# Entropy-model transfers with 16 rows outermost, and a result step moved behind the attention maxima

## What is computed

```python
# layer 0: attention over positions; c = 192, q and k have 24 channels
q, k, v = prelu(conv1x1(gn(x), w))            # three weights
score = softmax(einsum('bnc,bcm->bnm', q, k), axis=2)
x = x + einsum('bnm,bmc->bnc', score, v)      # "x2" below
# layer 1: an entropy model, per channel, on lower = gn(x) - 0.5 and upper = gn(x) + 0.5
for i in range(4):                             # 1 -> 3 -> 3 -> 3 -> 1 hidden values per channel
    logits = softplus(m[i]) @ logits + b[i]
    if i < 3: logits = logits + tanh(f[i]) * tanh(logits)
sign = -sign(lower + upper)
x = x + max(abs(sigmoid(sign * upper) - sigmoid(sign * lower)), 1e-6)
```

## Time and profile before

| | before |
|---|---|
| median of 3 runs | 5420.98 us |
| the profiled execution | 5410.94 us |
| its span on the core | 5409.1 us |
| PE busy | 84% |
| DVE busy | 80% |
| ACT busy | 67% |
| POOL busy | 18% |
| mean DMA rate | 56 GB/s |

### The profile page before, as it was taken

The page is one execution under the profiler, slowest core; times in us unless marked ns, Lnnn a source line. Parts: engine busy times, 40 slices in busy tenths (PEclk is TensorE's granted clock), DMA queues, the critical chain, the costliest instruction groups (busy, mean ns, idle before and its releaser), DMA issues.

```text
span 5409.1 us, 104827 instructions
## 1 busy us (share of the span) xinstructions
PE 4526.1 (84%) x38408; PEld 3015.6 (56%) x38408; DVE 4302.0 (80%) x5570; ACT 3613.2 (67%) x3912; POOL 967.5 (18%) x942
## 2 busy tenths in 40 slices
PE   4999679996899968998689986899769997699955
PEld 2887237771377614775157851678416783177711
DVE  4897589975899768996789967898678986789755
ACT  1666676666766667666766667667676676766666
POOL 4000311113111130112211032110311103111023
PEclk8999899998999989999899988999889998899977
DMA  2101330013300132002321023101331003301132
GB/s 58 25 19 36 101 89 28 24 45 102 83 24 29 51 105 73 24 26 67 107 56 31 27 73 107 44 28 33 82 97 46 24 30 92 110 23 31 31 97 80
DMA packets 107361, 305.15 MB, mean 56 GB/s; under 512 B 14401, under 2 KB 14785, under 8 KB 105090
## 3 DMA queue, kind: packets, MB, share of 16 engines
q1 hardware_dynamic: 106818, 298.01, 19.8%
HBM read 230.65 MB, written 50.33 MB: 52 GB/s over the span
## 4 chain that ended last, share of the span: by engine, by line
PE 48%; DVE 19%; issue 12%; DMA 9%; ACT 7%; SPq 4%; DVEq 0%; POOL 0%; ACTq 0%; POOLq 0%
PE ps L1295 9%; PE ps L1297 9%; PE ps L1299 9%; DMA arena<-x2d 7%; PE ps L1086 6%; DVE mxp L992 5%; PE ps L1247 5%; DVE arena L987 4%; ACT th L654 3%; DVE th L931 3%; PE ps L1158 3%; ACT arena L647 2%; PE ps L1172 2%; DMA qst<-shared 2%; SPq L333 2%
## 5 line engine op out<-in xcount | busy, mean ns | idle before, releaser
L1295 PE MATMUL ps<-v_sb,arena 128*128 128x193 f16 x8192 | 2020.0, 247 | 11.4 <-DVE arena L987 11.4
L1297 PE MATMUL ps<-v_sb,arena 128*128 128x192 f16 x8192 | 2028.7, 248 | 0.0
L1299 PE MATMUL ps<-v_sb,arena 128*128 128x193 f16 x8192 | 2012.1, 246 | 0.0
L612 ACT ACTIVATE arena<-ps 128x1024 f16<-128x1024 f32 x1024 | 1050.6, 1026 | 1022.4 <-PE ps L1086 1022.3
L987 DVE TENSOR_TENSOR arena<-arena 128x1024 f16<-128x1024 f32 x1024 | 1318.6, 1288 | 244.1 <-ACT arena L615 243.5
L931 DVE SCALAR_TENSOR_TENSOR th<-th,gates,ps 128x1024 f32<-128x1024 f32 x768 | 954.7, 1276 | 440.4 <-ACT th L654 437.4
L992 DVE TENSOR_REDUCE mxp<-ps 128x1 f32<-128x512 f32 x1792 | 1171.6, 685 | 49.1 <-PE ps L1247 40.0
L654 ACT ACTIVATE th<-ps,biases 128x1024 f32<-128x1024 f32 x768 | 827.9, 1114 | 478.5 <-PE ps L1158 417.8
L615 ACT ACTIVATE arena<-ps 128x1024 f32<-128x1024 f32 x1024 | 1045.8, 1021 | 0.0
L1297 PEld LDWEIGHTS ps<-v_sb,arena 128*128 128x128 f16 x8192 | 795.7, 97 | 262.0
L1295 PEld LDWEIGHTS ps<-v_sb,arena 128*128 128x128 f16 x8192 | 792.9, 97 | 143.5 <-issue 19.3
(11 more groups left out here) (119 smaller groups left out, 3519.3 us busy)
## 6 DMA issues: line engine op xcount, KB each, us to landing
x<-x2d SPq DMA_DIRECT2D x384, 256.0 KB
arena<-x2d SPq DMA_DIRECT2D x384, 128.0 KB, 3.8
xp<-x_dram SPq DMA_DIRECT2D x18, 1536.0 KB, 12.7
shared<-x_dram SPq DMA_DIRECT2D x64, 384.0 KB, 3.5
x2d<-shared SPq DMA_DIRECT2D x64, 384.0 KB, 3.0
res<-x2d SPq DMA_DIRECT2D x384, 64.0 KB
out_dram<-res SPq DMA_DIRECT2D x96, 256.0 KB
kst<-shared SPq DMA_DIRECT2D x32, 256.0 KB, 11.5
```

What stands on the lines that cost most here:

```text
L612: act.activation(e_hi[:, q % 4, :].rearrange("p (k n) -> p k n", k=2), sc, ACT.Exp)
L1295: pe.matmul(acc, eh, v_sb[:, m, 0:C + 1], start=(m == 0 and t % 2 == 0), stop=False, skip_group_check=True)
L1297: pe.matmul(acc[:, 0:C], eh, v_sb[:, m, VW:VW + C], start=False, stop=False, skip_group_check=True)
L1299: ins = pe.matmul(acc, el, v_sb[:, m, 0:C + 1], start=False, stop=(m == MT - 1), skip_group_check=True)
```

## The change

`load_x4` writes only the 48 rows (times 2) that the first tanh needs, in 6 transfers of 16 partitions, in place of 2 of 64; the rows 48 to 63 of each half are set to 0 once, at the start. `load_side` becomes 4 transfers of 16 partitions and one copy each, in place of 2 with two copies. `load_res` becomes 1 transfer over 128 partitions with 8 outermost, in place of 4. `x2d` is in the natural order of the blocks, so that a chunk of 1024 positions is two pieces of 2 KB, 4 KB apart. In phase B `result` is at p = 15. The waits on the semaphores follow the counts.

```diff
+X4_DMAS = 2 * 3
+SIDE_DMAS = 2 * 2
...
-PLACE = (0, 2, 1, 3, 4, 6, 5, 7)
...
-                sp.dma_start(x2d[bass.ds(row, C), PLACE[j] * N:(PLACE[j] + 1) * N].rearrange("(h p) n -> p h n", h=2),
+                sp.dma_start(x2d[bass.ds(row, C), j * N:(j + 1) * N].rearrange("(h p) n -> p h n", h=2),
                              xr[:, j % 2, :, :]).then_inc(x2_stored[j % 2], 16)
+
+            def part(row, v, a):
+
+                half = x2d[bass.ds(row + v // 2 * UC, UC), v % 2 * 2 * HC:(v % 2 + 1) * 2 * HC]
+                return half.rearrange("c (k a n) -> a c k n", a=2, n=N)[a]

             def load_x4(row, v):
                 for a in range(2):
-                    col = (v % 2 * 2 + a) * HC
-                    sp.dma_start(x4[64 * a:64 * a + 64, v % X4R, :],
-                                 x2d[bass.ds(row + v // 2 * UC, UC), col:col + HC].unsqueeze(0)
-                                 .to_broadcast([4, UC, HC])).then_inc(x4_in[v % X4R], 16)
+                    for i in range(HID):
+                        first = 64 * a + UC * i
+                        sp.dma_start(x4[first:first + UC, v % X4R, :].rearrange("p (k n) -> p k n", n=N),
+                                     part(row, v, a)).then_inc(x4_in[v % X4R], 16)
...
                 for a in range(2):
-                    col = (v % 2 * 2 + a) * HC
-                    sp.dma_start(t0[64 * a + 48:64 * a + 64, v % T0R, :, :],
-                                 x2d[bass.ds(row + v // 2 * UC, UC), col:col + HC].unsqueeze(1)
-                                 .to_broadcast([UC, 2, HC])).then_inc(side_in[v % T0R], 16)
+                    for d in range(2):
+                        sp.dma_start(t0[64 * a + 48:64 * a + 64, v % T0R, d, :].rearrange("p (k n) -> p k n", n=N),
+                                     part(row, v, a)).then_inc(side_in[v % T0R], 16)
+
+            def chunked(dram, row, u):
+                return dram[bass.ds(row + u * UC, UC), :].rearrange("c (k n) -> k c n", n=N)

             def load_res(l, row, u):
...
-                for g in range(4):
-                    chunks = x2d[bass.ds(row + u * UC, UC), g // 2 * 2 * HC:(g // 2 + 1) * 2 * HC]
-                    sp.dma_start(res[32 * g:32 * g + 32, u % XR, :],
-                                 chunks.rearrange("c (a k n) -> k a c n", a=2, n=N)[g % 2]).then_inc(res_in[u % XR], 16)
+                sp.dma_start(res[:, u % XR, :], chunked(x2d, row, u)).then_inc(res_in[u % XR], 16)
...
+            pool.memset(x4[:, :, :], 0.0)
             pool.memset(v_sb[:, :, C:VW], 1.0).then_inc(set_gp, 1)
...
-                        if l is not None and j < LATER and p == 10:
+                        if l is not None and j < LATER and p == PAIRS - 1:
                             result(l, UNITS - LATER + j)
```

More of the change, by code:

```diff
@@ L330, in load_res @@
                 sp.wait_ge(stored[u % XR], freed)
-                for g in range(4):
-                    chunks = x2d[bass.ds(row + u * UC, UC), g // 2 * 2 * HC:(g // 2 + 1) * 2 * HC]
-                    sp.dma_start(res[32 * g:32 * g + 32, u % XR, :],
-                                 chunks.rearrange("c (a k n) -> k a c n", a=2, n=N)[g % 2]).then_inc(res_in[u % XR], 16)
+                sp.dma_start(res[:, u % XR, :], chunked(x2d, row, u)).then_inc(res_in[u % XR], 16)
             def store(l, row, u):
                 sp.wait_ge(res_ready, l * UNITS + u + 1)
-                sp.dma_start(out_rows[bass.ds(row + u * UC, UC), :].rearrange("c (k n) -> k c n", n=N), res[:, u % XR, :]).then_inc(stored[u % XR], 16)
+                sp.dma_start(chunked(out_rows, row, u), res[:, u % XR, :]).then_inc(stored[u % XR], 16)
             def phase_a(l, row, proj):
@@ L641, in first_tanh @@
                     if d == 0:
-                        act.wait_ge(x4_in[v % X4R], l * (HALVES // X4R) * 32 + 32 * (v // X4R + 1))
+                        act.wait_ge(x4_in[v % X4R], l * (HALVES // X4R) * X4_DMAS * 16 + X4_DMAS * 16 * (v // X4R + 1))
                         if v >= T0R:
@@ L897, in result @@
                 dve.wait_ge(size_ready, l * UNITS + u + 1)
-                dve.wait_ge(res_in[u % XR], (l * (UNITS // XR) + (u // XR + 1)) * 4 * 16)
+                dve.wait_ge(res_in[u % XR], l * (UNITS // XR) * 16 + (u // XR + 1) * 16)
                 dve.scalar_tensor_tensor(res[:, u % XR, :], half, 1e-6, res[:, u % XR, :], ALU.max, ALU.add
@@ L1149, in first_layer @@
                     if d == 0:
-                        pe.wait_ge(side_in[v % T0R], l * (HALVES // T0R) * 32 + (v // T0R + 1) * 32)
+                        pe.wait_ge(side_in[v % T0R], l * (HALVES // T0R) * SIDE_DMAS * 16 + (v // T0R + 1) * SIDE_DMAS * 16)
                     tanh_done = pe.compute_val(l * SLOTS + s + 1)
```

## The result

| | before | changed |
|---|---|---|
| median | 5422.43 us (4 runs) | 5095.93 us (4 runs, 5090.35 to 5108.31) |
| ratio | | 0.9403, 95% interval 0.9383 to 0.9424 |
| the profiled execution | 5410.94 us | 5108.31 us |
| its span | 5409.1 us | 5106.5 us |
| mean granted clock of PE | 0.942 | 0.972 |

The change makes the kernel 6.0% faster. The profiled execution of the changed kernel is the slowest of its four; between the two traces 302.6 us are gone. The profiled execution before lies 11.5 us under its median, the changed one 12.4 us over its own, so the medians differ by 24 us more, 326.5 us. In the changed kernel the lines are 7 higher from the second layer's tanh on: L647, L654, L931, L1158, L1172 and L1231 of before are now L654, L661, L938, L1165, L1179 and L1238. On SP, `load_x4` is L318, `load_side` L329, `load_res` L339, `store` L343, `stack` L354.

The account below looks back on a forecast made before the run. Phase A was taken to wait for `load_side` behind few-outermost transfers crowding a few DMA engines, attention to be bound by PE and DVE. 259 + 54 + 18 = 331 us off 5410.94 gave 5080 us, range 5020 to 5200.

Parts of the forecast that it names:

- the forecast's own: Whole kernel: the case of 5020 to 5150 us, given chance 0.78.
- Phases A with projections: Seven phases A: the waits for `load_side` go, 41 us an image less 4 for what remains, 37 x 7 = 259 us gained.
- the 4 held back for waits: Phase A: 4 us an image charged for halves and stacks where side data still land too late for PE.
- small waits: First part of phase A, 1205 to 1321 us: 2 us added to ACT's busy time within the 86 us forecast.
- The chain's own idle time: Phase A: ACT idles 0.9 us in each unit behind DVE's result, charged for 4 units in the first part.
- Last phase A: Last phase A: ACT's 161.71 us busy plus idle make 175 of 233; 58 gained, less 4, so 54 us.
- `load_side` in four: Phase A: side data land some 4.5 us after the tanh, 0.8 us later than a free pair; PE needs them at 5.5.
- SP's load: SP in phase A: issues take 5.7 us against a half of 7 to 8 us, so they fit and cost 0.
- Both rivals of SP: SP's issues bound phase A: mildly at 0.72 us each, 5270, chance 0.04; slower kernel from about 0.8 us, 6450 at 1.28, chance 0.04.
- `result` at p = 15: Attention, 42 blocks: 1.32 us given back at p = 11, 0.9 paid before `denominators`; net 0.42 each, 18 us gained.
- Byte rival: Phase A is bound by bytes at 102 to 104 GB/s; a half moves 896 KB, before 1024: about 5170 us, chance 0.12.
- Signs that were wrong: Among signs named for a right prediction: first-layer waits under 40 us, ACT over 90% busy, PE clock near 1.00, DMA share no higher.

Follow-up runs that it names:

- The pair with 4 and 16 outermost: Changed kernel with `load_x4` loading all 64 rows in 2 KB pieces: 4 broadcast transfers with 4 outermost, 5233.11 us; 8 with 16 outermost, 5130.53 us.
- `load_res` runs: Changed kernel with `load_res` as 4 transfers with 2 outermost, 5169.00 us, or as 2 transfers with 4 outermost, 5142.38 us.
- `result` moved: Changed kernel with phase A's `result` two slots later, after the gates of slots s = 4k + 2 in place of 4k: 5101.73 us.
- the stacks: Changed kernel with stack transfers two at a time in the even halves, none in the odd ones: 5084.77 us.
- The other layout: Kernel before, its `x2d` order and 4 KB pieces kept; `load_x4` in 6 transfers, `load_res` in 8, all loads 16 outermost, `result` at p = 15: 5093.81 us.

## Why the prediction was right

5080 was forecast, 5096 measured, inside 5020 to 5200, and the case that came is the forecast's own. Against the profiled execution the sum had 331 us; the traces differ by 303, the medians by 326.5. So the total came out within 5 us by medians, and of what falls short in the traces, below, up to 24 us may be the scatter of the two profiled executions. That nearness is in part luck, for the phases A with projections gave less than forecast and attention more.

**The bound.** That the work of few-outermost transfers crowded the queue, and that `load_side` landed late behind it, was argued from the pushback on SP and the low DMA share. The pair with 4 and 16 outermost, with the `load_res` runs, shows it; the low share was no evidence for it (last section). What the Trainium skill ("DMA: Bandwidth & Descriptors", "Why a DMA increments its semaphore by 16 and not by 1") states on the number of engines agrees with these runs in direction, and with the counts of small packets. The rule of the Trainium skill on the same page ("Rules for kernel authors") that small transfers should be coalesced did not decide here: 8 transfers of 64 KB beat 4 of 128 KB by 103 us.

**Phases A with projections, 259 us forecast, 223 measured.** This term came out too large in the traces, by 5.2 us an image. About 0.9 of it is that the stretches of image 1 were taken for all seven: image 1 itself gains 32.7 us where 37 were forecast. The part before slot 22 was to take 86 us, plus most of the 4 held back for waits, and takes 91.5 in the mean. ACT's waits there, in image 1 of the changed kernel:

```profile
ACT th L661 <- PE ps L1165: 6.2, 5, 2.2
ACT lu L642 <- PE ps L1148: 1.9, 3, 0.9
ACT lu L632 <- POOL lu L522: 1.7, 1, 1.7
ACT lu_sign L627 <- POOL lu_sign L516: 1.4, 2, 1.1
```

The last three come to 5.0 us, where the sum had 2 us for "small waits". The trace of before already has 4.6 us of them in its stretch (2.4, 1.7 and 0.5). This is a term that was clearly mis-sized. The chain's own idle time was set low as well, but by little: the 0.92 us of the earlier trace rows is 1.11 in seven of the units of the changed kernel's last phase A, and 1.39 and 1.72 at most:

```profile
4937.78 2.30 ACT L661 ACTIVATE th<-ps,biases 128x1024 f32<-128x1024 f32 x2 [1.11 <-PE ps L1165]
...
5015.13 2.12 ACT L661 ACTIVATE th<-ps,biases 128x1024 f32<-128x1024 f32 x2 [1.39 <-PE ps L1165]
```

That it was shorter before because ACT was catching up after a stall is possible and not shown. `result` moved gave 2.7 us in this part, the stacks 0.8. The slots with maxima gained 8.2 us an image (75.4 to 67.2) where 9.4 were forecast from a stretch that was 11 us shorter, the end 0.9 where it was 2.

**Last phase A, 54 forecast, 54 measured.** ACT's work plus a small gap per unit was the right model where no projections run: 17.4 us of idle time were allowed, the 4 for waits included, and 18.3 are there.

**`load_side` in four.** It was to land some 4.5 us after the tanh; in the last phase A it lands 3.8 to 4.6 us after the tanh in all halves but one, so in time. Where the projections run it is later at times: 6.6 to 8.8 us in halves 4, 8, 10 and 12 of image 1, past the 5.5 that the prediction gave it. The other layout shows that splitting it has no price that can be told.

**SP's load, 0 forecast.** Right: 0.372 us an issue. Both rivals of SP needed 0.72 us or more. In SP's own waits those for the tanh (ACT L654) still come to 502.6 us, so it has time in hand.

**`result` at p = 15, 18 forecast, 25 to 30 measured.** The 1.32 us given back are 1.32 at five of the six blocks and 1.43 at one. The 0.9 us paid are 0.59 at the first block change and 0.76 to 0.85 at the five others (`low` to `low`), as steps that follow each other without a wait start closer together than their durations add up to: from the start of `low` at 1520.00 to `denominators` at 1523.13 four steps with durations of 3.25 us take 3.13.

**Byte rival, 5170, chance 0.12.** Refuted, by 125 GB/s and by the run that moves 1024 KB a half in 5131 us.

**Signs that were wrong.** Of those named for a right prediction, the first layer's waits came to 43.5 us (under 40 was said), ACT is 87% busy in the first part (over 90), PE's clock is 0.94 to 0.97 in most of phase A (near 1.00), and the DMA share rose from 0.38 to 0.48 (it was to be no higher). The last is a false reading of the share, taken up below.

## What to carry to other kernels

Look at the outermost size of every transfer, and first at the large ones with a small outermost size, such as a leading broadcast: here no engine waited for `load_x4` itself, and changing it alone gave 241 us, for it delayed the short transfers issued behind it. Signs in the profile were a landing far above the least of the same line, issues of the same form that sometimes take several times their median, and both beside a DMA share far from full. Size the small waits from the trace as well; they do not go with the large one. A step moved off a full engine is worth what it gives back less what it delays where it lands; both sides can be read from the trace of before.

## What was not expected of the hardware

The DMA share was no measure of crowding here. With the same bytes and the same pieces, the queue's share over the span was 20.3% with 4 outermost and 22.9% with 16, in a kernel 103 us faster (queue, kind: packets, MB, share of 16 engines; first 4 outermost, then 16):

```profile
q1 hardware_dynamic: 151362, 298.04, 20.3%
```

```profile
q1 hardware_dynamic: 172866, 298.13, 22.9%
```

The time of the packets, in the mean over 16 engines, is 1063 us with 4 outermost and 1175 with 16 (the share times the span of 5235.0 and 5129.0 us), while the transfers land earlier. The share moves by about a point with nothing changed in the transfers but their order, too: 21.4% in the changed kernel, 20.5% with the stacks in even halves.

And SP's cost of an issue goes with the form of the transfer rather than with its size. With 16 outermost the median is 0.366 us at 128 KB (`load_side` before) and 0.372 at 64 KB; with 4 outermost it is 0.557 at 128 KB and 0.580 at 256 KB (`load_x4` with 4 outermost, and before); with 8 outermost 0.706 at 256 KB, with 2 outermost 0.631 at 64 KB (`load_res`).
